# Conditioned attention on one core: the last three of 32 steps written out with four score banks, and the opening in another order

## The chip, the cores and the metric

The kernel runs on one core of one Trainium2 chip. The metric is the device time of one execution in microseconds (us), lower is better. The median of three runs before the change is 683.97 us (683.66 to 684.18).

## The reference

For each of 8 batch entries `x` is 512 tokens by 512 features, in 16 heads of 32. A condition vector is projected with the same weights and added to queries and keys (not to values). All in float32.

```python
Q = _split_heads(x @ Wq.T + bq)
K = _split_heads(x @ Wk.T + bk)
V = _split_heads(x @ Wv.T + bv)
cQ = Q + _split_heads(tokens @ Wq.T + bq)
cK = K + _split_heads(tokens @ Wk.T + bk)
scores = jnp.einsum('bhqd,bhkd->bhqk', cQ, cK) / jnp.sqrt(jnp.float32(HEAD_DIM))
attn = jax.nn.softmax(scores, axis=-1)
out = jnp.einsum('bhqk,bhkd->bhqd', attn, V)
x = x + out
```

## The kernel before, in words

**Tiling.** A group `g` is one batch entry and four heads, G = 32 groups. Everything is kept with features on the partitions. A projection is 12 products of 128x512: the float32 operand is split into a high part (rounded, `Wh`, `Xh`) and a low part (the rest, `Wl`, `Xl`), and high by high, low by high and high by low are added up over four chunks. The projected Q and K are split again into `hi` (`qk_hi`, ACT) and `lo` (`qk_lo`, DVE), and DMAs on SP's queue (`stack`) lay these out as rows of `Qs` and `Ks`, in three slots. A score tile then is one product over 96 rows.

**A group's work.** (1) `maxima`: 16 products of 128x512 in turn into two PSUM banks `MXB`, and on DVE one `row_maxima` each (L538), to find each query's maximum. POOL splits the maxima (`parts`), DVE turns them (`maxima_turned`), and four DMAs (`maxima_rows`, L757) put them under the queries as two more rows. (2) `scores`: 16 products over 98 rows (L291) in turn into two banks `STB`; ACT writes the exponentials to `Pt` (`exps`, L454), chunk by chunk of keys, four heads to a chunk. (3) `values`: per key chunk four products of V by `Pt` (L306), 16 in all and each recorded twice, into a bank of `OB`. (4) The sums: POOL adds the four chunks of `Pt` to `A` (`add`, L692, three additions of 128x2048), DVE `key_sums` reduces A (L551), PE `totals` (L314) finishes them. (5) DVE finishes: `sums_inverted`, `inverse_turned`, `normalised`, `added` (L559, L570, L580, L589), and SP stores.

**Order.** Every engine's order is written out by hand, and engines wait for each other on semaphores only. Step `t` of the loop interleaves on PE the 16 scores of group t with 16 maxima that are 9 tiles ahead of group t+1's beginning, with the 36 products of the three projections of group t+3, and, after score 1, with `totals(t-2)` and all of `values(t-1)`. From step 29 (G - 3) on there are no projections, and in steps 30 and 31 few or no maxima; the loop goes on as it is, with special code in step 31 (`last_adds`, `last_values`, `last_sums`), where the sums of the last group come from ones-products on PE. The projections' two banks `RB` are not used in these steps.

**Opening.** It projects q0, k0, q1, k1 one after the other, with the small `condition` and `condition_sum` products between, then interleaves 25 maxima tiles with v0, v1, v2, q2 and k2. The ACT order is L456 to L489, the DVE order L601 to L627. The weight chunks 2 and 3 of Wq and Wk are loaded on SP's queue (L788) and cast on ACT by `w_hi` (L406). `qk_hi(1, 1)` stands ahead of these casts (L477), and `qk_lo(1, 1)` behind the third row maximum (`K1_LO_AT`, L620).

## Time and profile before

| | |
|---|---|
| median of 3 runs | 683.97 us (683.66 to 684.18) |
| profiled execution | 683.72 us, its span 681.9 us |
| PE, DVE, POOL, ACT busy | 666.1, 542.1, 491.1, 376.0 us |
| mean granted clock of PE | 0.985 of full speed |
| chain that ended last | PE 92%, DMA 3%, DVE 2% |

PE is TensorE (PEld its weight loads), DVE VectorE, ACT ScalarE, POOL GpSimd, SP the engine whose queue issues the DMAs. A row of the timeline gives the start in the span, the duration, the engine, the line and operation, what is written from what, and in brackets how long the engine stood idle before and who released it. A row with xN merges N neighbours. The chain is followed back from the last instruction to what released it.

### The profile page before, as it was taken

The numbers are of one execution on the slowest core, as the hardware profiler recorded it, in microseconds if no ns is written. First come the engines' busy times: TensorE is split into PE (matmuls) and PEld (weight loads), VectorE is DVE, ScalarE is ACT, GpSimd is POOL, SyncE is SP. The second block draws the span as 40 slices with busy tenths as digits, with TensorE's granted clock in tenths as the row PEclk, the third lists the DMA queues.
The fourth block names the chain that finished last, engine by engine and source line by source line (L and its number), as shares of the span: only waits on it lengthen the run. The fifth ranks groups of instructions, "written<-read, shape, count | busy, mean of one in ns | idle before, by whom it ended". The sixth has DMA issues, their size and how long they took to land.

```text
span 681.9 us, 10057 instructions
## 1 busy us (share of the span) xinstructions
PE 666.1 (98%) x3534; PEld 451.0 (66%) x3534; DVE 542.1 (80%) x819; ACT 376.0 (55%) x659; POOL 491.1 (72%) x205
## 2 busy tenths in 40 slices
PE   8999999999999999999999999999999999999976
PEld 6776677666677666667766666776666677665521
DVE  4676888888888888888888888888888888888836
ACT  6335655555566555555655555565555555555552
POOL 6518777778877777887777798777779776667880
PEclk9999999999999999999999999999999999999878
DMA  7944334555343455533345553334554333444111
GB/s 242 237 109 99 89 105 100 139 140 141 99 116 98 109 139 140 134 101 112 100 116 141 139 129 99 112 96 127 140 140 121 82 97 91 123 125 125 33 48 46
DMA packets 48274, 79.85 MB, mean 117 GB/s; under 512 B 9824, under 2 KB 9824, under 8 KB 48224
## 3 DMA queue, kind: packets, MB, share of 16 engines
q1 hardware_dynamic: 47696, 79.19, 43.6%
q8 instruction: 28, 0.46, 0.3%
q14 instruction: 22, 0.18, 0.1%
q10 hardware_dynamic: 528, 0.02, 0.0%
HBM read 19.95 MB, written 8.39 MB: 42 GB/s over the span
## 4 chain that ended last, share of the span: by engine, by line
PE 92%; DMA 3%; DVE 2%; ACT 1%; SPq 1%; issue 1%; ACTq 0%; DVEq 0%
PE bank L198 25%; PE bank L291 18%; PE bank L276 17%; PE bank L306 16%; PE bank L254 13%; PE bank L314 1%; DVE mf L538 1%; ACT Pt L454 1%; DMA Ks<-lo 1%; DMA xr<-xT 1%; PE bank L323 1%; DMA cT<-condT 1%; DMA Qs<-mt 1%; SPq L757 0%; SPq L744 0%
## 5 line engine op out<-in xcount | busy, mean ns | idle before, releaser
L454 ACT ACTIVATE Pt<-bank 128x512 f32<-128x512 f32 x512 | 301.6, 599 | 238.2 <-PE bank L291 157.1
L538 DVE TENSOR_REDUCE mf<-bank 128x1 f32<-128x512 f32 x512 | 344.8, 686 | 106.6 <-PE bank L276 105.4
L692 POOL TENSOR_TENSOR A<-A,Pt 128x2048 f32<-128x2048 f32 x62 | 284.6, 4590 | 4.9
L291 PE MATMUL bank<-Qs,Ks 98*128 98x512 f32 x512 | 212.4, 417 | 4.6 <-ACT Pt L454 2.8
L276 PE MATMUL bank<-Ks,Qs 96*128 96x512 f32 x512 | 208.5, 407 | 1.8 <-DMA Ks<-lo 1.3
L692 POOL TENSOR_TENSOR A<-Pt 128x2048 f32<-128x2048 f32 x31 | 142.9, 4609 | 4.0 <-DVE part_sums L551 4.0
L291 PEld LDWEIGHTS bank<-Qs,Ks 98*128 98x128 f32 x512 | 97.6, 191 | 69.8 <-ACT Pt L454 46.4
L674 POOL TENSOR_TENSOR Xl<-xr,Xh 128x512 fp32r<-128x512 f32 x28 | 36.1, 1292 | 119.6 <-ACT Xh L422 119.6
L276 PEld LDWEIGHTS bank<-Ks,Qs 96*128 96x128 f32 x512 | 97.6, 191 | 28.4 <-DVE mf L538 5.2
L306 PE MATMUL bank<-Pt,V 128*32 128x512 f32 x992 | 114.2, 600 | 0.0
L198 PE MATMUL bank<-Xl,Wh 128*128 128x512 f32 x256 | 102.4, 400 | 0.0
L198 PE MATMUL bank<-Xh,Wl 128*128 128x512 f32 x256 | 102.1, 399 | 0.0
L198 PE MATMUL bank<-Xh,Wh 128*128 128x512 f32 x256 | 101.9, 398 | 0.0
L551 DVE TRANSPOSE_TENSOR_REDUCE part_sums<-A 128x32 f32<-128x1024 f32 x62 | 76.4, 1234 | 5.9 <-POOL A L692 5.9
L306 PEld LDWEIGHTS bank<-Pt,V 128*32 128x32 f32 x992 | 34.6, 110 | 52.7 <-issue 52.7
L198 PEld LDWEIGHTS bank<-Xh,Wh 128*128 128x128 f32 x256 | 48.9, 191 | 12.1 <-issue 0.8
L198 PEld LDWEIGHTS bank<-Xh,Wl 128*128 128x128 f32 x256 | 49.0, 192 | 11.2
L198 PEld LDWEIGHTS bank<-Xl,Wh 128*128 128x128 f32 x256 | 49.1, 192 | 10.8
L529 DVE SCALAR_TENSOR_TENSOR lo<-bank,tb,hi 128x512 fp32r<-128x512 f32 x64 | 47.6, 743 | 6.3 <-ACT hi L437 6.3
L254 PE MATMUL bank<-Wl,Xh 128*128 128x512 f32 x128 | 51.0, 399 | 0.0
L254 PE MATMUL bank<-Wh,Xl 128*128 128x512 f32 x128 | 51.0, 399 | 0.0
L254 PE MATMUL bank<-Wh,Xh 128*128 128x512 f32 x128 | 50.4, 394 | 0.0
(55 smaller groups left out, 328.5 us busy)
## 6 DMA issues: line engine op xcount, KB each, us to landing
Qs<-hi SPq DMA_DIRECT2D x64, 256.0 KB, 3.6
Ks<-hi SPq DMA_DIRECT2D x64, 256.0 KB, 3.6
Qs<-lo SPq DMA_DIRECT2D x32, 256.0 KB, 4.1
Ks<-lo SPq DMA_DIRECT2D x32, 256.0 KB, 4.0
res<-xT SPq DMA_DIRECT2D x32, 256.0 KB, 2.9
outT<-ot SPq DMA_DIRECT2D x32, 256.0 KB, 3.8
xr<-xT SPq DMA_DIRECT2D x28, 256.0 KB, 2.7
Qs<-mt SPq DMA_DIRECT2D x128, 4.0 KB
```

Source lines behind the costliest of these rows:

```text
L198: m = e.matmul(ring_bank(use)[:, :], w[:, qk, c, kc * P:(kc + 1) * P], x[:, b % 2, kc, :], start=(n == 0), stop=(n == 11))
L254: m = e.matmul(ring_bank(use)[:, :], x[:, b % 2, kc, c * P:(c + 1) * P], w[:, 2, kc, :], start=(n == 0), stop=(n == 11))
L276: e.matmul(MXB[u % 2][:, :], Qs[0:96, sl, j, qc * P:(qc + 1) * P], Ks[0:96, sl, j, :], start=True, stop=True).then_inc(t_mx, 1)
L291: e.matmul(STB[u % 2][:, :], Ks[0:98, sl, j, kc * P:(kc + 1) * P], Qs[0:98, sl, j, :], start=True, stop=True).then_inc(t_st, 1)
L306: m = e.matmul(OB[g % 2][32 * j:32 * j + 32, :], V[:, b % 2, kc, h * HD:(h + 1) * HD], Pt[:, kc, j, :], start=(kc == 0), stop=(kc == KC - 1))
L314: m = e.matmul(bk[32 * j:32 * j + 32, 0:16], sel[:, :], part_sums[:, j, :], start=True, stop=True)
L454: e.activation(Pt[:, kc, j, :], STB[u % 2][:, :], ACT.Exp, scale=SCALE).then_inc(a_e, 1)
L529: e.scalar_tensor_tensor(lo[:, qk, :], ring_bank(("qk"[qk], g))[:, :], tb[:, qk, c, b:b + 1], hi[:, qk, :].bitcast(F32), ALU.add, ALU.subt ...
L538: e.reduce_max(mf[:, g % 2, 4 * j + qc:4 * j + qc + 1], MXB[u % 2][:, :], AXX).then_inc(v_mx, 1)
L551: e.tensor_reduce(part_sums[:, 2 * i:2 * i + 2, :].rearrange("p j n -> p (j n)"), A[:, 2 * i:2 * i + 2, :].rearrange("p j (n i) -> p (j n) ...
L674: e.tensor_tensor(Xl[:, b % 2, kc, :], xr[:, n % 2, :], Xh[:, b % 2, kc, :].bitcast(F32), ALU.subtract).then_inc(p_x, 1)
L692: e.tensor_tensor(A[:, :, :], Pt[:, 0, :, :] if kc == 1 else A[:, :, :], Pt[:, kc, :, :], ALU.add).then_inc(p_a, 1)
```

## The change

The opening: on PE `condition_sum(1, 0)` comes after product 5 of k0's projection, not after 8. On ACT `qk_hi(1, 1)` comes after the four `w_hi` casts, on DVE `qk_lo(1, 1)` right after its bias and ahead of all row maxima.

The last three steps leave the loop and are written out. In step 29 all 23 maxima tiles that remain are done, two to a score. From group 30 on scores go to four banks (`STB` and `RB`). The value products of groups 29, 30 and 31 run in halves or smaller. The sums of groups 30 and 31 come from ones-products (`last_sums`): one addition on DVE (`add_first`) of chunks 0 and 1, and three ones-products per head. The sums of groups 29 and 31 are held in the part of `V` that is no longer needed; the residual rows of groups 30 and 31 are loaded early into `hi` and `xr`, and the last output has a buffer of its own. On DVE `key_sums` of group 28 comes after step 29's maxima.

```diff
@@ -20,7 +20,6 @@
 SCALE = float(HD) ** -0.5
 FIN = 4
 WARM = 3
-K1_LO_AT = 2
@@ -35,7 +34,11 @@
 Q_LO_AT, K_LO_AT = 11, 17
 FINISH_AT = (1, 1, 1, 1)
 SUMS_AT = (4, 6)
-LAST_AT = (9, 10, 11, 12)
+TAIL_MAXIMA = (1, 1, 2, 2, 2, 2, 2, 2, 2, 2, 2, 2, 1, 0, 0, 0)
+EARLY_AT, LATE_AT, LAST_SUMS_AT = 11, 3, 6
...
@@ -153,6 +156,24 @@
         def freed(use):
             kind, g = use
             return {"q": (v_lo, 2 * g + 1), "k": (v_lo, 2 * g + 2), "v": (a_v, g + 1)}[kind]
+        def st_bank(u):
+            return (STB + RB)[u % 4] if u >= SLOTS * (G - 2) else STB[u % 2]
+        def added_up(g):
+            return V[:, 0, :, :] if g in (G - 3, G - 1) else A
+        def res_rows(g):
+            if g < G - 2:
+                return res[:, :]
+            return hi[:, 0, :].bitcast(F32) if g == G - 2 else xr[:, 0, :]
+        def out_rows(g):
+            return ot[:, :] if g < G - 1 else xr[:, 1, :]
         def st_unit(g, kc, j):
...
@@ -284,20 +305,25 @@
                     if g < NSLOT:
                         e.wait_ge(p_ks, g + 1)
                 u = SLOTS * g + n
-                if u >= 2:
+                if u < 2:
+                    e.wait_ge(a_tc, 5 + u)
+                elif u < SLOTS * (G - 2) + 2:
                     e.wait_ge(a_e, u - 1)
+                elif u < SLOTS * (G - 2) + 4:
+                    e.wait_ge(v_lo, 2 * G)
+                    e.wait_ge(a_v, G)
                 else:
-                    e.wait_ge(a_tc, 5 + u)
-                e.matmul(STB[u % 2][:, :], Ks[0:98, sl, j, kc * P:(kc + 1) * P], Qs[0:98, sl, j, :],
+                    e.wait_ge(a_e, u - 3)
+                e.matmul(st_bank(u)[:, :], Ks[0:98, sl, j, kc * P:(kc + 1) * P], Qs[0:98, sl, j, :],
                          start=True, stop=True).then_inc(t_st, 1)
-            def values(g):
+            def values(g, chunks):
                 b, c = divmod(g, KC)
-                if g >= 2:
+                if g >= 2 and chunks[0] == 0:
                     e.wait_ge(v_f, finished(g - 2, FIN))
                 if g == 0:
                     e.wait_ge(v_tb, 6)
-                for kc in range(KC):
+                for kc in chunks:
                     if c == 0:
                         e.wait_ge(a_v, KC * b + kc + 1)
...
@@ -314,26 +340,18 @@
                     m = e.matmul(bk[32 * j:32 * j + 32, 0:16], sel[:, :], part_sums[:, j, :], start=True, stop=True)
                 m.then_inc(t_l, 1)
...
+                    m = e.matmul(bk[32 * j:32 * j + 32, :], ones[:, :],
+                                 added_up(g)[:, j, :] if kc is None else Pt[:, kc, j, :],
+                                 start=(kc is None), stop=(kc == KC - 1))
                 if kc == KC - 1:
-                    m.then_inc(t_last, 1)
-            def last_sums():
-                e.wait_ge(v_a, 2)
-                for j in range(4):
-                    e.matmul(MXB[1][32 * j:32 * j + 32, :], ones[:, :], A[:, j, :], start=True, stop=False)
-                e.wait_ge(a_e, st_unit(G - 1, KC - 1, 3))
-                for j in range(4):
-                    m = e.matmul(MXB[1][32 * j:32 * j + 32, :], ones[:, :], Pt[:, KC - 1, j, :],
-                                 start=False, stop=True)
-                m.then_inc(t_last, 1)
+                    m.then_inc(t_l, 1)
             warm_up()
@@ -345,7 +363,7 @@
             condition(1, 0)
             for n in range(12):
                 project_qk(1, 0, n)
-                if n == 8:
+                if n == 5:
                     condition_sum(1, 0)
             condition(0, 1)
             condition(1, 1)
@@ -372,32 +390,61 @@
             for k, g, n in first[done:]:
                 project(k, g, n)
...
-                    if u < SLOTS * G:
-                        maxima(u, t - 2 if n == VALUES_AT + 1 and t >= 2 else None)
+                    maxima(u, t - 2 if n == VALUES_AT + 1 and t >= 2 else None)
                     for k, g, i in work[done:done + PROJ[n]]:
                         project(k, g, i)
                     done += PROJ[n]
                     if n == VALUES_AT and t >= 1:
                         if t >= 2:
-                            e.wait_ge(v_mx, min(u, SLOTS * G))
+                            e.wait_ge(v_mx, u)
                             totals(t - 2, MXB[(u + 1) % 2])
-                        values(t - 1)
-                    if t == G - 1 and n == LAST_AT[0]:
-                        e.wait_ge(v_f, finished(G - 3, 1))
-                        totals(G - 2, MXB[0])
-                    if t == G - 1 and n == LAST_AT[3]:
-                        last_values(0)
-                        last_values(1)
-            last_values(2)
-            last_sums()
-            last_values(3)
+                        values(t - 1, range(KC))
+            u = SLOTS * (G - 2) + MAX_LEAD
+            for n in range(SLOTS):
+                scores(G - 3, n)
+                for i in range(TAIL_MAXIMA[n]):
+                    maxima(u, G - 5 if n == VALUES_AT + 1 and i == 0 else None)
+                    u += 1
+                if n == VALUES_AT:
+                    e.wait_ge(v_mx, u - 1)
+                    totals(G - 5, MXB[u % 2])
+                    values(G - 4, range(KC))
+                if n == EARLY_AT + 1:
+                    values(G - 3, (0, 1))
+            for n in range(SLOTS):
+                scores(G - 2, n)
+                if n == LATE_AT:
+                    values(G - 3, (2, 3))
+                    e.wait_ge(v_mx, SLOTS * G)
+                    totals(G - 4, MXB[0])
+                if n == EARLY_AT:
+                    values(G - 2, (0, 1))
+            for n in range(SLOTS):
+                scores(G - 1, n)
+                if n == LATE_AT:
+                    values(G - 2, (2, 3))
+                    e.wait_ge(v_f, finished(G - 4, 1))
+                    totals(G - 3, MXB[0])
+                if n == LAST_SUMS_AT:
+                    for kc in (None, 2, 3):
+                        last_sums(G - 2, MXB[1], kc)
+                if n == EARLY_AT:
+                    values(G - 1, (0, 1))
+            values(G - 1, (2,))
+            e.wait_ge(v_f, finished(G - 3, 1))
+            for kc in (None, 2, 3):
+                last_sums(G - 1, MXB[0], kc)
+            values(G - 1, (3,))
...
@@ -449,9 +496,14 @@
                 u = SLOTS * g + n
                 if j == 0 and g >= 1:
                     e.wait_ge(t_pv, KC * (g - 1) + kc + 1)
-                    e.wait_ge(p_a, 3 * (g - 1) + max(kc, 1))
+                    if g == G - 1 and kc < 2:
+                        e.wait_ge(v_a, 1)
+                    elif g == G - 1:
+                        e.wait_ge(t_l, G - 1)
+                    else:
+                        e.wait_ge(p_a, 3 * (g - 1) + max(kc, 1))
                 e.wait_ge(t_st, u + 1)
-                e.activation(Pt[:, kc, j, :], STB[u % 2][:, :], ACT.Exp, scale=SCALE).then_inc(a_e, 1)
+                e.activation(Pt[:, kc, j, :], st_bank(u)[:, :], ACT.Exp, scale=SCALE).then_inc(a_e, 1)
             e.wait_ge(v_c, 1)
             e.dma_start(cT[:, :, 0:B], condT).then_inc(d_c, 16)
@@ -474,10 +526,10 @@
             wv_hi(2)
             wv_hi(3)
             qk_hi(0, 1)
-            qk_hi(1, 1)
             for c in (2, 3):
                 w_hi(0, c)
                 w_hi(1, c)
+            qk_hi(1, 1)
             copy_part(0, 2)
             copy_part(1, 2)
...
@@ -558,11 +610,11 @@
                     e.wait_ge(v_f, finished(g - 1, FIN))
                 e.reciprocal(rc[:, :], bk[:, 0:16]).then_inc(v_f, 1)
-            def last_sums_inverted():
-                e.wait_ge(t_last, 1)
...
             def added(g):
                 O = OB[g % 2]
                 c = g % KC
                 e.wait_ge(v_f, finished(g, 3))
-                e.wait_ge(d_res, 16 * (g + 1))
-                if g >= 1:
+                if g < G - 2:
+                    e.wait_ge(d_res, 16 * (g + 1))
+                else:
+                    e.wait_ge(d_res_last, 32)
+                if 1 <= g < G - 1:
                     e.wait_ge(d_out, 16 * g)
-                e.scalar_tensor_tensor(ot[:, :], O[:, :], bqk[:, 2, c:c + 1], res[:, :],
+                e.scalar_tensor_tensor(out_rows(g), O[:, :], bqk[:, 2, c:c + 1], res_rows(g),
                                        ALU.add, ALU.add).then_inc(v_f, 1)
-            def last_adds(kc):
-                if kc == 1:
-                    e.wait_ge(v_s, 2 * (G - 1))
-                e.wait_ge(a_e, st_unit(G - 1, kc, 3))
-                if kc == 2:
-                    e.wait_ge(v_a, 1)
-                e.tensor_tensor(A[:, :, :], Pt[:, 0, :, :] if kc == 1 else A[:, :, :], Pt[:, kc, :, :],
-                                ALU.add).then_inc(v_a, 1)
+            def add_first(g):
+                e.wait_ge(v_s, 2 * (g - 1) if g == G - 1 else 2 * (G - 3))
+                e.wait_ge(a_e, st_unit(g, 1, 3))
+                e.tensor_tensor(added_up(g)[:, :, :], Pt[:, 0, :, :], Pt[:, 1, :, :], ALU.add).then_inc(v_a, 1)
             e.memset(cT[:, :, :], 0.0).then_inc(v_c, 1)
...
@@ -613,12 +661,9 @@
             for g in (0, 1):
                 for qk in (0, 1):
                     bias(qk, g)
-                    if (qk, g) != (1, 1):
-                        qk_lo(qk, g)
+                    qk_lo(qk, g)
             for u in range(SLOTS + MAX_LEAD):
                 row_maxima(u)
-                if u == K1_LO_AT:
-                    qk_lo(1, 1)
                 if u in (7, 8):
                     bias(u - 7, 2)
                 if u == SLOTS + 3:
@@ -626,11 +671,9 @@
             for qk in (0, 1):
                 qk_lo(qk, 2)
-            for t in range(G):
+            for t in range(G - 3):
                 for n in range(SLOTS):
-                    u = SLOTS * (t + 1) + n + MAX_LEAD
-                    if u < SLOTS * G:
-                        row_maxima(u)
+                    row_maxima(SLOTS * (t + 1) + n + MAX_LEAD)
                     if (g := due(t, n, TURN_AT, 1, 1)) is not None:
                         maxima_turned(g)
...
-                            normalised(G - 2)
-                        if n == LAST_AT[3]:
-                            added(G - 2)
-                        if n == 15:
-                            last_adds(2)
-            last_sums_inverted()
+            u = SLOTS * (G - 2) + MAX_LEAD
+            for n in range(SLOTS):
+                for i in range(TAIL_MAXIMA[n]):
+                    row_maxima(u)
+                    u += 1
+                if n == VALUES_AT:
+                    sums_inverted(G - 5, MXB[u % 2])
+                    inverse_turned(G - 5)
+                    normalised(G - 5)
+                    added(G - 5)
+                    qk_lo(1, G - 1)
+                if n == 6:
+                    maxima_turned(G - 2)
+            maxima_turned(G - 1)
+            key_sums(G - 4, 0)
+            key_sums(G - 4, 1)
+            sums_inverted(G - 4, MXB[0])
+            inverse_turned(G - 4)
+            normalised(G - 4)
+            added(G - 4)
+            add_first(G - 2)
+            key_sums(G - 3, 0)
+            key_sums(G - 3, 1)
+            sums_inverted(G - 3, MXB[0])
+            inverse_turned(G - 3)
+            normalised(G - 3)
+            added(G - 3)
+            last_sums_inverted(G - 2, MXB[1])
+            inverse_turned(G - 2)
+            add_first(G - 1)
+            normalised(G - 2)
+            added(G - 2)
+            last_sums_inverted(G - 1, MXB[0])
             inverse_turned(G - 1)
             normalised(G - 1)
...
@@ -684,12 +748,15 @@
                                 ALU.subtract).then_inc(p_ml, 1)
             def add(g, kc):
-                if kc == 1 and g >= 1:
+                if kc == 1 and g == G - 3:
+                    e.wait_ge(t_pv, KC * (G - KC))
+                elif kc == 1 and g >= 1:
                     e.wait_ge(v_s, 2 * g)
                 if kc > 1:
                     e.wait_ge(p_a, 3 * g + kc - 1)
                 e.wait_ge(a_e, st_unit(g, kc, 3))
-                e.tensor_tensor(A[:, :, :], Pt[:, 0, :, :] if kc == 1 else A[:, :, :], Pt[:, kc, :, :],
+                sums = added_up(g)
+                e.tensor_tensor(sums[:, :, :], Pt[:, 0, :, :] if kc == 1 else sums[:, :, :], Pt[:, kc, :, :],
                                 ALU.add).then_inc(p_a, 1)
             e.memset(sel[:, :], 0.0).then_inc(p_sel, 1)
@@ -715,16 +782,21 @@
             parts(0)
             x_lo(1, 2)
-            for t in range(G):
+            for t in range(G - 3):
                 if t >= 1:
                     add(t - 1, 3)
                 b, kc = divmod(t + 3, KC)
                 if b + 1 < B:
                     x_lo(b + 1, kc)
-                if t < G - 1:
-                    parts(t + 1)
-                    add(t, 1)
-                    add(t, 2)
+                parts(t + 1)
+                add(t, 1)
+                add(t, 2)
+            add(G - 4, 3)
+            parts(G - 2)
+            add(G - 3, 1)
+            parts(G - 1)
+            add(G - 3, 2)
+            add(G - 3, 3)
...
@@ -765,14 +837,17 @@
             def load_res(g):
                 b, c = divmod(g, KC)
-                if g >= 1:
+                if g >= G - 2:
+                    e.wait_ge(d_st[(G - 1) % NSLOT][0], 16 * 3 * ((G - 1) // NSLOT + 1))
+                    e.wait_ge(p_x, KC * (B - 1))
+                elif g >= 1:
                     e.wait_ge(v_f, finished(g - 1, FIN))
-                e.dma_start(res[:, :], xT[b, c * P:(c + 1) * P, :]).then_inc(d_res, 16)
+                e.dma_start(res_rows(g), xT[b, c * P:(c + 1) * P, :]).then_inc(d_res if g < G - 2 else d_res_last, 16)
...
                 if t >= 2:
                     store(t - 2)
-                if t + 1 < G:
-                    maxima_rows(t + 1)
-            for g in (G - 2, G - 1):
-                load_res(g)
+                maxima_rows(t + 1)
+            load_res(G - 4)
+            maxima_rows(G - 1)
+            load_res(G - 2)
+            load_res(G - 1)
+            store(G - 4)
+            load_res(G - 3)
+            for g in (G - 3, G - 2, G - 1):
                 store(g)
             e.wait_ge(d_out, 16 * G)
```

## Rows read from the trace of the kernel before

**Rows 1.** The page: the chain that ended last, and POOL's additions (section 5).
```profile
PE 92%; DMA 3%; DVE 2%; ACT 1%; SPq 1%; issue 1%; ACTq 0%; DVEq 0%
L692 POOL TENSOR_TENSOR A<-A,Pt 128x2048 f32<-128x2048 f32 x62 | 284.6, 4590 | 4.9
```
**Rows 2.** Timeline, the value products of four steps.
```profile
602.14 3.64 PE L306 MATMUL bank<-Pt,V 128*32 128x512 f32 x32
622.12 3.64 PE L306 MATMUL bank<-Pt,V 128*32 128x512 f32 x32
639.77 3.64 PE L306 MATMUL bank<-Pt,V 128*32 128x512 f32 x32
654.77 5.02 PE L306 MATMUL bank<-Pt,V 128*32 128x512 f32 x32
```
**Rows 3.** Timeline, waits in the last three steps.
```profile
626.47 1.97 DVE L538 TENSOR_REDUCE mf<-bank 128x1 f32<-128x512 f32 x3 [0.83 <-PE bank L276]
630.35 0.77 PE L276 MATMUL bank<-Ks,Qs 96*128 96x512 f32 x1 [1.11 <-DMA Ks<-lo]
632.54 0.79 PE L276 MATMUL bank<-Ks,Qs 96*128 96x512 f32 x1
653.49 1.22 PE L291 MATMUL bank<-Qs,Ks 98*128 98x512 f32 x2 [1.51 <-DMA Qs<-mt]
656.75 1.09 ACT L454 ACTIVATE Pt<-bank 128x512 f32<-128x512 f32 x2 [4.13 <-PE bank L306]
```
**Rows 4.** Stretches: us, then engines' busy time, PEclk (granted clock), DMA share, GB/s.
```profile
630.00:631.00 1.00, 0.65 (x2) 0.58 (x3) 1.00 (x3) 0.00 (x0) 0.17 (x1) 0.66 0.05 18
637.00:638.00 1.00, 1.00 (x4) 0.43 (x2) 0.98 (x2) 0.79 (x2) 1.00 (x1) 0.92 0.04 6
650.00:651.00 1.00, 0.73 (x2) 0.34 (x2) 0.00 (x0) 0.94 (x2) 1.00 (x1) 0.90 0.00 0
657.00:658.00 1.00, 1.00 (x12) 0.29 (x8) 0.55 (x1) 0.84 (x2) 1.00 (x1) 0.68 0.00 0
30.00:40.00 10.00, 10.00 (x44) 8.10 (x44) 8.60 (x14) 1.72 (x3) 1.71 (x3) 1.00 0.22 51
```
**Rows 5.** Timeline of the opening, ACT's `qk_hi(1, 0)`.
```profile
14.12 0.69 ACT L437 ACTIVATE hi<-bank,tb 128x512 fp32r<-128x512 f32 x1 [1.07 <-PE bank L198]
```
**Rows 6.** Timeline of the opening: weight loads, casts, `qk_hi(1, 1)`, maxima, `qk_lo(1, 1)`.
```profile
16.72 0.61 SPq L732 DMA_DIRECT2D Pt<-wqT  x1
18.34 0.44 SPq L732 DMA_DIRECT2D Pt<-wkT  x1
20.96 0.69 ACT L437 ACTIVATE hi<-bank,tb 128x512 fp32r<-128x512 f32 x1 [2.39 <-DMA Ks<-lo]
21.55 2.62 ACT L406 ACTIVATE Wh<-Pt 128x512 fp32r<-128x512 f32 x4
22.53 0.40 PE L276 MATMUL bank<-Ks,Qs 96*128 96x512 f32 x1
23.57 0.74 DVE L529 SCALAR_TENSOR_TENSOR lo<-bank,tb,hi 128x512 fp32r<-128x512 f32 x1
```
**Rows 7.** DMA issues of 16.6 to 18.6: KB each, median us to landing.
```profile
Pt<-wqT SPq DMA_DIRECT2D x2, 256.0 KB, 4.9
```
**Rows 8.** Timeline, pace of maxima and exps, the end of step 29, DVE's addition.
```profile
619.16 3.38 DVE L538 TENSOR_REDUCE mf<-bank 128x1 f32<-128x512 f32 x5 [0.16 <-PE bank L276]
637.21 1.12 ACT L454 ACTIVATE Pt<-bank 128x512 f32<-128x512 f32 x2 [0.26 <-PE bank L291]
645.14 4.74 ACT L454 ACTIVATE Pt<-bank 128x512 f32<-128x512 f32 x8 [0.18 <-PE bank L291]
665.86 2.29 DVE L598 TENSOR_TENSOR A<-Pt 128x2048 f32<-128x2048 f32 x1
```
**Rows 9.** The chain that ended last, near its end: start, us, what.
```profile
674.35 0.86 PE bank L331 x8
676.13 0.73 DVE rr L564
```

More of the change, by code:

```diff
@@ L95, in cond_attention @@
         d_res = sem("d_res")
+        d_res_last = sem("d_res_last")
         d_out = sem("d_out")
@@ L373, in tensor_program @@
                 project(k, g, n)
-            for t in range(G):
-                work = [(k, t + 3, n) for k in "vqk" if t + 3 < G for n in range(12)]
+            for t in range(G - 3):
+                work = [(k, t + 3, n) for k in "vqk" for n in range(12)]
                 done = 0
@@ L551, in key_sums @@
                 e.tensor_reduce(part_sums[:, 2 * i:2 * i + 2, :].rearrange("p j n -> p (j n)"),
-                                A[:, 2 * i:2 * i + 2, :].rearrange("p j (n i) -> p (j n) i", i=32), AXX, ALU.add,
+                                added_up(g)[:, 2 * i:2 * i + 2, :].rearrange("p j (n i) -> p (j n) i", i=32), AXX, ALU.add,
                                 apply_transpose=True).then_inc(v_s, 1)
@@ L716, in pool_program @@
             x_lo(1, 2)
-            for t in range(G):
+            for t in range(G - 3):
                 if t >= 1:
@@ L774, in store @@
                 e.wait_ge(v_f, finished(g, FIN))
[L775 removed]
+                e.dma_start(outT[b, c * P:(c + 1) * P, :], out_rows(g)).then_inc(d_out, 16)
             load_x0(0)
@@ L798, in sync_program @@
             stack(1, 2)
-            for t in range(G):
+            for t in range(G - 2):
                 b, kc = divmod(t + 3, KC)
@@ L805, in sync_program @@
                     load_res(t - 2)
-                if t >= 1 and t + 2 < G:
+                if t >= 1:
                     stack(0, t + 2)
```

34 lines of the change are left out of this document (11 added, 23 removed).

## The prediction, made before the changed kernel ran

> **What bounds the kernel now.** I read the page first. The matrix engine (PE) holds 92% of the chain that ended last [rows 1], so one step of the loop lasts as long as PE's own work. The timeline gives its length: the 32 records of the value products start at 602.14 and again at 622.12 [rows 2], a step of 19.98 us. In this regime no other engine's saving shows. That leaves the two ends, where PE is not the limit all the time. I read both as timelines and then as one-microsecond stretches for the granted clock.
>
> In the last three steps the projections are over. Value products start at 622.12, 639.77 and 654.77 [rows 2], so the steps are 17.7 and 15.0 us, and the rest from 654.77 to the span's end takes 27.1. Each time they run, ACT, which has two score banks only, runs dry: 4.13 us before 656.75 [rows 3]. PE also idled 1.11 us for the K rows of the last group before 630.35, and 1.51 for the maxima rows before 653.49 [rows 3]. And its clock fell three times to half (1.2 GHz): in the stretches that begin at 630 and 650, and it came back at 637 and 657 [rows 4]; a third fall, at 664 to 671, looks the same. Each lasted some 7 us.
>
> **The opening (three edits).** The moved `condition_sum(1, 0)` runs three matmuls earlier. Its consumer, `qk_hi(1, 0)` at 14.12, is released by the projection's end and not by the bias [rows 5]. I cost it at nothing; the cover is the projection itself. If the copy that it reads were late, PE would wait up to the 0.7 us of the three matmuls.
>
> `qk_hi(1, 1)` goes behind four casts of weight chunks on ACT. Now it runs at 20.96 and the casts take 2.62 us from 21.55 [rows 6]. Could the casts run in ACT's idle time before 20.96? No: their loads are issued from 16.72 to 18.34 [rows 6] and take 4.9 us to land [rows 7], which is 21.6 for the first and 23.2 for the last. So the casts stay where they are and end at 24.17, and `qk_hi(1, 1)`, 0.69 long, ends at 24.86 instead of 21.65.
>
> `qk_lo(1, 1)` on DVE goes from behind three row maxima to ahead of all of them. Queued behind its wait are all 25 row maxima of group 0 and the start of group 1, and PE waits for these: maxima tile 2 uses the bank of tile 0. On DVE the lower part takes 0.74 [rows 6], so it ends at about 25.65, the first maximum at 26.34, and PE's third maxima product goes from 22.53 [rows 6] to 26.4: **+3.9 us**. Nothing gives this back. From 30 to 40 PE is busy 10.00 of 10 us [rows 4], and the whole loop hangs on it by the step length above.
>
> The stall has a second price. PE would stand about 3.7 us. In the tail a stand of 1.11 us after sparse scores was enough for the clock to be at half when it went on [rows 3, 4]. PE then works at half rate where it is the bound. If the fall comes during the stall and ends near 33, 6.6 us run at half rate: **+3.3 us**. Bounds: the fall from 650 to 657 ended 3.0 us after PE's dense run of value products began at 654.77 [rows 3, 4], which would be +1.5 here; two falls in a row would be +6.6, and no fall would be 0. I take +3.3 because this stretch is not dense either: `condition` and `condition_sum`, small products that wait for copies, cut into it. Opening together: **+7.2 us** (3.9 to 10.5).
>
> The Trainium skill ("TensorE: Matmul & The Clock Gate", section "HAM oscillation — how this bites in real kernels") says that a wait between groups of matmuls can throttle the array, so that the next group starts cold. The trace agrees at 630 [rows 4]. By a reading that only the wait itself counts, the opening would cost 3.9; by the rule, the sum above.
>
> **The tail (one rewrite).** I walk it from 626.04, up to which nothing changes, in the old kernel's times. Step 29 now holds all 23 remaining maxima tiles instead of 16. From 626.47 [rows 3] on DVE has 21 to do; back to back one costs 0.68 (3.38 for five [rows 8]).
>
> - Five are done by 629.9. The next is the first of group 31 and waits for the same K rows as before: PE idles again till 630.35, and the clock falls again.
> - At half clock two banks give a reduction about every 0.78 us: the 0.79 of a product after a wait [rows 3], 0.69 for its reduction, 0.08 of hand-over, over two banks. Sixteen take from 631.2 to about 643.7 (643.0 at full clock).
> - The price: scores are interleaved one to two maxima. PE comes to the first half of `values(29)` at 642.8. At half clock a half takes 3.5 us (the full one 3.64 at full clock [rows 2]), so score 13 starts at 646.3 and the exps of step 29 end at 648.7. Before, they ended at 638.3 [rows 8]. The step is 10 us longer.
> - From there ACT can run nearly without a gap: eight exps take 4.74 us [rows 8], 9.5 for a step, against 15.0 now. Four banks cover 2.4 us of PE's absence and a half of the values is 1.8 at full clock. With `totals(28)` and the latency of the next score ACT idles 0.8 in step 30. It idles 0.4 behind the second half in step 31, and 1.5 at `last_sums(30)`: twelve ones-products, each group of four 0.86 [rows 9], stand between scores 6 and 7.
> - ACT's exps for step 30 then start at 648.7, and the last of step 31 ends at 671: 32 at 0.59, and 2.7 to 3.5 of such gaps.
> - The end: `last_sums` for chunk 3 comes 1.6 us behind the last exp, as PE still has the values of chunk 2 and two groups of sums to do. From the transposition to the end of the span it was 5.8 us (676.13 to 681.9 [rows 9]) and stays that. The span of the tail ends at 678.2: **-3.7 us**.
>
> Covers. POOL: `add(29, 2)` goes behind `parts(31)`, so it starts at 644 and the third addition ends at 653.3 (4.59 each [rows 1]); exp 12 of step 30 waits for it and comes at 655, cover 1.7. DVE: `add_first(30)`, 2.29 [rows 8], is needed by the first exp of step 31 (659) and ends at 657. The score rows for group 31 are there about 4 us behind the last reduction, at 648, seven before they are used. SP: `load_res(30)` and `load_res(31)` stand ahead of `store(28)` and `load_res(29)`, all waits behind them long over; buffers `hi` and `xr` are idle then, cost nothing. The other output rows cost nothing.
>
> Bounds of the tail: at full clock from 640 on, -5.4 (676.5). If the clock stays at half through the second half of `values(29)` too, the exps of step 29 end 0.5 later and ACT's gap behind that half is 3.2 instead of 0.8: 681.1, a gain of 0.8 only.
>
> The Trainium skill ("SBUF — State Buffer", "Who interferes with whom") says that a VectorE instruction with two SBUF inputs contends with a GpSimd instruction that reads SBUF. No row here shows the two at once: the two DVE additions of the tail (2.29 and 2.28) started after POOL's last one had ended. With it the sum would grow by what the third rival below gives.
>
> **The sum.** +7.2 - 3.7 = +3.5. The profiled execution took 683.72 (span 681.9, 1.8 around it), 0.25 below the median of 683.97. So 687.2 against its own time, 687.4 against the median.
>
> **Rivals.**
> - *The clock holds in the opening, and the tail runs at full clock* (the side of faster). Place: PE's stall at 22.7 to 26.4. Price 3.9 only; the tail's rewrite gives 5.4. That is -1.5: 682.4. Against it: all three sparse stretches of the tail lost the clock [rows 4]. It decides from the point where the opening costs less than the tail gives. Chance 0.13. With the tail at -3.7 it is +0.2, 684.2: no change, chance 0.12.
> - *Long half-clock spells, or late sums.* The opening costs 10.5, or the tail gives 0.8. Step 29 is then the bound that replaced PE: DVE's 21 reductions push everything behind them. +6.4 to +9.7: 690.4 to 693.7. For it: at half clock PE has more to do per exp and misses more of them, as at 650 to 657 [rows 4]; against it: the dense values end such a spell. Chance 0.2.
> - *DVE and POOL get in each other's way.* `add_first(30)` at 654 meets a late `add(29, 3)`: up to 2.3 more on DVE, of which the 2 us of cover take most; then the sums of group 29 come late at `totals(29)`: +1 to +2, 689. Chance 0.05, worked out from the DVE row of 2.29 and the POOL row of 4.59 [rows 1]. The rule of the Trainium skill quoted above is this one.
> - *The change does not do what it says*: ACT still runs dry at each block of values because bank four comes too late. Tail 0, total +7.2: 691.2, counted with the second rival.
>
> **How the numbers follow.** The forecast, 685.4 to 690.4 (the opening's low bound with the likeliest tail, up to one spell more), has 0.5 and is the likeliest. Faster by over 0.2% is below 682.6 and slower is above 685.3 (about what a measurement of this kernel can tell from no change). Faster 0.13, same 0.12, slower 0.75. The range leaves out the worst of the long spells and the best of the first rival: 682.5 to 692.0.
>
> **What would show it.** In the opening: the third maxima product at 26.4 instead of 22.5, `qk_hi(1, 1)` behind the casts at 24.2, matmuls at 0.63 instead of 0.40 till about 33, and the value products of every later step shifted by one constant. If they are shifted by less than 3, the DVE or landing term fails; if by 4, the clock term. In the tail: a last reduction near 643.5 plus the shift, steps 30 and 31 of about 11 us each, ACT almost gapless in them, and the distance from the value products of step 29 (622.12 now) to the end of the span 3.7 us shorter than 59.8. The forecast is wrong if the casts find their loads landed early, or if the tail, paced by DVE and not by PE, holds the clock.

## The result, and the profile after

The changed kernel takes 687.53 us (median of 5 runs, 686.1 to 688.28) against 684.18 for the old one: ratio 1.0045, 95% interval 1.0027 to 1.0062. It is slower, by 3.35 us; forecast were +3.5 and 687.4. Line numbers are those of each kernel: L297 is the maxima product (L276 before), L317 the score (L291), L332 the value product (L306), L506 the exp (L454).

The page of the changed kernel, span and chain:

```profile
span 686.5 us, 10100 instructions
PE 94%; DMA 2%; DVE 1%; ACT 1%; SPq 1%; issue 0%; ACTq 0%
```

The opening in its timeline (start, duration, engine, line, operation, idle time and releaser), to be laid beside [rows 6]:

```profile
21.84 0.40 PE L297 MATMUL bank<-Ks,Qs 96*128 96x512 f32 x1
25.19 0.63 ACT L453 ACTIVATE Wh<-Pt 128x512 fp32r<-128x512 f32 x1 [0.48 <-DMA Pt<-wkT]
25.73 0.67 ACT L484 ACTIVATE hi<-bank,tb 128x512 fp32r<-128x512 f32 x1
26.43 0.75 DVE L581 SCALAR_TENSOR_TENSOR lo<-bank,tb,hi 128x512 fp32r<-128x512 f32 x1 [6.82 <-ACT hi L484]
27.10 1.28 DVE L590 TENSOR_REDUCE mf<-bank 128x1 f32<-128x512 f32 x2
27.84 0.80 PE L297 MATMUL bank<-Ks,Qs 96*128 96x512 f32 x1 [5.13 <-DVE mf L590]
```

This is the chain of the forecast, read from top to bottom: the last cast waits for its load, the high part of k1 stands behind the cast, the low part waits 6.82 us on DVE, the row maxima stand behind it, and PE's third maxima product starts at 27.84 instead of 22.53 after standing 5.13 us. The loads were slower than before. The DMA view of the same stretch, KB each and median us to landing:

```profile
Pt<-wqT SPq DMA_DIRECT2D x2, 256.0 KB, 5.9
```

That is 1.0 more than [rows 7], and the stall is 1.4 longer than forecast (27.84 - 22.53 = 5.3 against 3.9). The clock, by stretches of one microsecond (PEclk is the third number from the end; compare [rows 4]):

```profile
25.00:26.00 1.00, 0.00 (x0) 0.00 (x0) 0.00 (x0) 0.81 (x2) 1.00 (x2) 0.95 1.08 227
32.00:33.00 1.00, 1.00 (x10) 0.20 (x8) 0.46 (x1) 0.00 (x0) 0.00 (x0) 0.63 0.06 25
636.00:637.00 1.00, 0.09 (x1) 0.00 (x0) 0.81 (x2) 0.36 (x1) 0.12 (x1) 0.94 0.77 256
653.00:654.00 1.00, 1.00 (x6) 0.50 (x2) 0.61 (x1) 0.00 (x0) 1.00 (x1) 0.52 0.03 4
```

It fell to half during the stall, at 25.9, and came back at 32.7. In the tail it fell at 636.9, and came back only at 654: one spell of 17 us in place of three of 7.

The tail in the timeline, beside [rows 2, 3, 8]:

```profile
629.22 3.64 PE L332 MATMUL bank<-Pt,V 128*32 128x512 f32 x32
637.07 0.77 PE L297 MATMUL bank<-Ks,Qs 96*128 96x512 f32 x1 [0.98 <-DMA Ks<-lo]
646.03 1.36 PE L297 MATMUL bank<-Ks,Qs 96*128 96x512 f32 x2
649.75 3.64 PE L332 MATMUL bank<-Pt,V 128*32 128x512 f32 x16
654.14 1.08 ACT L506 ACTIVATE Pt<-bank 128x512 f32<-128x512 f32 x2 [4.04 <-PE bank L317]
659.38 4.03 ACT L506 ACTIVATE Pt<-bank 128x512 f32<-128x512 f32 x8 [1.30 <-PE bank L317]
664.39 4.03 ACT L506 ACTIVATE Pt<-bank 128x512 f32<-128x512 f32 x8 [0.98 <-PE bank L317]
672.98 2.56 ACT L506 ACTIVATE Pt<-bank 128x512 f32<-128x512 f32 x5 [1.95 <-PE bank L317]
676.54 2.07 ACT L506 ACTIVATE Pt<-bank 128x512 f32<-128x512 f32 x4 [1.00 <-PE bank L317]
680.75 0.72 DVE L616 STREAM_TRANSPOSE rr<-bank 128x512 f32<-128x512 f32 x1 [2.84 <-PE bank L350]
```

The value products of step 29 start at 629.22, 7.10 later than in [rows 2]: that is all that the opening costs. The first product of q2's projection, near the end of the opening, was 7.56 late, so 0.46 came back in between:

```profile
43.69 0.40 PE L219 MATMUL bank<-Xh,Wh 128*128 128x512 f32 x1
```

against this line of the old kernel:

```profile
36.13 0.40 PE L198 MATMUL bank<-Xh,Wh 128*128 128x512 f32 x1
```

From the value products of step 29 to the end of the span it is 57.3 us against 59.8 before: the tail gives 2.5. So +7.1 - 2.5 = +4.6, and the spans differ by 4.6 (686.5 and 681.9). Half of the value products (x16) now takes 3.64 us at 649.75, as long as all 32 records took before: half clock. Behind it ACT runs groups of eight exps in 4.03 us.

Two lengths carry the rest of this document. The **shift** is the start of the value products of step 29 less 622.12. The **tail** is the time from there to the end of the span.

### The profile page after: what moved, and what is told of

Read it like the earlier page. It is cut to its first block, busy times and chain, and to the rows that moved or that the text cites. A ratio compares the mean times of both kernels' runs of the same rounds, so it can differ in the third digit from the quotient of the medians.

```text
span 686.5 us, 10100 instructions
## 1 busy us (share of the span) xinstructions
PE 670.6 (98%) x3558; PEld 451.9 (66%) x3558; DVE 541.4 (79%) x818; ACT 374.6 (55%) x659; POOL 477.6 (70%) x202
## 4 chain that ended last, share of the span: by engine, by line
PE 94%; DMA 2%; DVE 1%; ACT 1%; SPq 1%; issue 0%; ACTq 0%
PE bank L219 26%; PE bank L317 19%; PE bank L297 18%; PE bank L332 16%; PE bank L275 13%; DMA Pt<-wkT 1%; PE bank L340 1%; PE bank L350 1%; DMA cT<-condT 1%; DVE mf L590 1%; DMA Ks<-lo 0%; SPq L816 0%; ACT hi L484 0%; PE bank L248 0%; ACT Pt L506 0%
## 5 line engine op out<-in xcount | busy, mean ns | idle before, releaser
L506 ACT ACTIVATE Pt<-bank 128x512 f32<-128x512 f32 x512 | 300.4, 600 | 236.9 <-PE bank L317 162.8
L759 POOL TENSOR_TENSOR A<-A,Pt 128x2048 f32<-128x2048 f32 x58 | 266.5, 4595 | 4.5
L297 PE MATMUL bank<-Ks,Qs 96*128 96x512 f32 x512 | 211.4, 414 | 7.0 <-DVE mf L590 5.8
L317 PE MATMUL bank<-Qs,Ks 98*128 98x512 f32 x512 | 208.1, 412 | 1.0 <-ACT Pt L506 0.6
L317 PEld LDWEIGHTS bank<-Qs,Ks 98*128 98x128 f32 x512 | 97.1, 191 | 63.7 <-ACT Pt L506 42.5
L759 POOL TENSOR_TENSOR A<-Pt 128x2048 f32<-128x2048 f32 x29 | 133.8, 4613 | 2.7 <-DVE part_sums L603 2.7
L297 PEld LDWEIGHTS bank<-Ks,Qs 96*128 96x128 f32 x512 | 98.7, 193 | 37.6 <-DVE mf L590 14.9
L332 PE MATMUL bank<-Pt,V 128*32 128x512 f32 x1024 | 119.0, 602 | 0.0
L603 DVE TRANSPOSE_TENSOR_REDUCE part_sums<-A 128x32 f32<-128x1024 f32 x58 | 71.5, 1234 | 0.0
L332 PEld LDWEIGHTS bank<-Pt,V 128*32 128x32 f32 x1024 | 35.0, 110 | 54.3 <-issue 52.7
```

What stands on the lines that cost most here:

```text
L297: e.matmul(MXB[u % 2][:, :], Qs[0:96, sl, j, qc * P:(qc + 1) * P], Ks[0:96, sl, j, :], start=True, stop=True).then_inc(t_mx, 1)
L317: e.matmul(st_bank(u)[:, :], Ks[0:98, sl, j, kc * P:(kc + 1) * P], Qs[0:98, sl, j, :], start=True, stop=True).then_inc(t_st, 1)
L332: m = e.matmul(OB[g % 2][32 * j:32 * j + 32, :], V[:, b % 2, kc, h * HD:(h + 1) * HD], Pt[:, kc, j, :], start=(kc == 0), stop=(kc == KC - 1))
L506: e.activation(Pt[:, kc, j, :], st_bank(u)[:, :], ACT.Exp, scale=SCALE).then_inc(a_e, 1)
L603: e.tensor_reduce(part_sums[:, 2 * i:2 * i + 2, :].rearrange("p j n -> p (j n)"), added_up(g)[:, 2 * i:2 * i + 2, :].rearrange("p j (n i) ...
L759: e.tensor_tensor(sums[:, :, :], Pt[:, 0, :, :] if kc == 1 else sums[:, :, :], Pt[:, kc, :, :], ALU.add).then_inc(p_a, 1)
```

## The experiments

`K1_LO_AT`, `TAIL_MAXIMA` and the other names are those of the diff above. Ratios are against the old kernel.

**1. The two parts alone.** One kernel is the old one with the three opening edits, the other the new one with them undone:

```diff
             qk_hi(0, 1)
-            qk_hi(1, 1)
             for c in (2, 3):
                 w_hi(0, c)
                 w_hi(1, c)
+            qk_hi(1, 1)
```

(and `qk_lo(1, 1)` ahead of the row maxima, `condition_sum(1, 0)` after product 5.)

> The old kernel with the three opening edits alone. My theory (the stall of the matrix engine at its third maxima product, and the half-clock spell behind it, shift everything): value products of every step about 7.0 us later than in the old kernel, 691.0 us in all. Rival (the opening costs only the wait, about 4, and the tail's rewrite loses the rest): 688. Second rival (the opening costs nothing, the loss is all in the tail): 684.

Measured: 690.54, ratio 1.009 (1.0065 to 1.0115). Shift 6.46, tail 59.5. The third maxima product starts at 26.25, 3.72 late.

> The new kernel with the old opening: only the last three steps are rewritten. My theory: the tail gives 2.5 us as in the changed kernel's profile (value products of step 29 to the end of the span: 57.3 against 59.8), so 681.5. Rival (the tail gives nothing or loses, the opening is cheap): 684 or more. If the two parts add up, this ratio and that of the opening alone sum to the change's.

Measured: 681.30, ratio 0.995 (0.993 to 0.9971). Shift 0.1, tail 57.3, as in the changed kernel. The two parts add up: +0.9% and -0.5% give the change's +0.45%. The rivals in which the opening is cheap or the tail gives nothing have fallen.

**2. Which of the opening's edits?** Old kernel with only the ACT order of the diff above:

> The old kernel with only the cast order on ScalarE changed: the high part of k1 behind the four weight casts; the low part stays behind the third row maximum. My theory: VectorE waits for the high part after three maxima instead of none, so the matrix engine stands at its sixth maxima product, not at the third, and gets three tiles and six value projections done first: +1.5 to +3, 685.5 to 687. Rival (the cost is the late landing of the high and low rows of K, not VectorE's order): +7, 691.

Measured: 684.59, ratio 1.0002 (0.9987 to 1.0017). Less than the 685.5 to 687 that I expected. The profile has the mechanism: the sixth maxima product waits for DVE, not the third.

```profile
26.46 0.75 DVE L529 SCALAR_TENSOR_TENSOR lo<-bank,tb,hi 128x512 fp32r<-128x512 f32 x1 [2.78 <-ACT hi L437]
27.86 0.50 PE L276 MATMUL bank<-Ks,Qs 96*128 96x512 f32 x1 [0.89 <-DVE mf L538]
```

In this timeline PE stands 0.89 us, its clock stays at 1.00, and the low part is just as late as in the changed kernel (26.46 and 26.43). This profiled execution's weight loads took 7.1 us to land, among the longest of all, and its shift of 1.6 is more than the medians show. Now only DVE's order:

```diff
                     bias(qk, g)
-                    if (qk, g) != (1, 1):
-                        qk_lo(qk, g)
+                    qk_lo(qk, g)
...
                 row_maxima(u)
-                if u == K1_LO_AT:
-                    qk_lo(1, 1)
```

> The old kernel with only VectorE's order changed: the low part of k1 ahead of all row maxima, its high part early as before. My theory: the high part ends at 21.7, so the first row maximum is 0.9 late and the third maxima product 0.6 late: 0 to +0.6, within 0.2% of the old kernel, 684.0 to 684.6. Rival (the low part's place alone makes the stall): +4 or more.

Measured: 685.61, ratio 1.002 (1.0005 to 1.0035), a little over what I expected. The third maxima product starts at 22.99, 0.46 late, and the shift is 0.58; its tail was 61.4 in this profile, with the same code as before. So the edits alone measured +0.02% and +0.2% (at most 0.35% by the interval), and all three together 0.9%. The late high part costs nothing that the medians show as long as three row maxima stand ahead of the low part; the early low part costs about half a microsecond by the shift as long as the high part is early. The loss is the pair. The third edit, `condition_sum`, is in the kernel with 0.9% as well and was not tried alone. The traces leave it little: the second maxima product, which comes after it, starts at 21.84 with it and at 21.81 without.

**3. The wait or the clock?** The opening edits with 20 products that nobody reads (`FILL` is 20) in PE's standing time:

```diff
             for u in range(SLOTS + MAX_LEAD):
+                if u == 2:
+                    for _ in range(FILL):
+                        e.matmul(OB[1][:, :], Wh[:, 0, 0, 0:P], Xh[:, 0, 0, :], start=True, stop=True)
                 maxima(u)
```

> The opening edits alone, with 20 products that nobody reads (into a free bank) before the third maxima product, 4.3 us of work in the time in which the matrix engine stands. My theory: the stall stays as long as it was (the third maxima product still waits for VectorE), but the clock stays at 2.4 GHz, which takes 2 to 3 us from the loss: 688.0 against 690.5 for the opening without them. Rival (the half-clock spell costs nothing, the whole loss is the wait): 690.5.

Measured: 687.88, ratio 1.0056 (1.0034 to 1.0077): 2.7 us below the opening without them by the medians, 2.3 by the ratios, 2.4 by the shift (4.10 against 6.46). The granted clock stayed at 1.00 from 20 to 38. From the third maxima product to the first product of q2's projection it was 13.6 us, exactly as in the old kernel, and 16.4 in the opening without fillers. The half-clock spell costs 2.8 us there and 2.3 in the changed kernel (15.85, from 27.84 to 43.69). In the opening without fillers that leaves the wait: 3.7 + 2.8 is its shift of 6.46. With the fillers the comparison of shifts understates the clock a little, since they ran longer than DVE kept PE waiting:

```profile
22.49 4.70 PE L366 MATMUL bank<-Xh,Wh 128*128 128x512 f32 x20
25.48 1.28 DVE L542 TENSOR_REDUCE mf<-bank 128x1 f32<-128x512 f32 x2
```

The first row maximum was done at 26.2, and the third maxima product started at 27.03, behind the last filler: about 0.8 us are the fillers' own.

**4. What are four banks worth?** The new tail with `st_bank` returning `STB[u % 2]` throughout:

```diff
-            return (STB + RB)[u % 4] if u >= SLOTS * (G - 2) else STB[u % 2]
+            return STB[u % 2]
```

(and the wait in `scores` back to `a_e >= u - 1`.)

> The new tail on the old opening, with two score banks for the last two groups instead of four. My theory: four banks cover 2.4 us of the matrix engine's absence at each block of values and let the exps run at 0.50 each, as the changed kernel's profile has it, not at 0.59: without them the last two steps grow by 1 to 2 us each, 684 to 685, and ScalarE's idle time before the first exp behind a block is over 2 us. Rival (the matrix engine is the bound there and the banks are idle luxury): 681.3, as with four.

Measured: 690.3, ratio 1.0075 (1.0051 to 1.0099), tail 66.7. Nine us more than with four banks (9.4 by the tail); I had expected three to four. Its profile says where. ACT in its timeline:

```profile
645.87 2.97 ACT L502 ACTIVATE Pt<-bank 128x512 f32<-128x512 f32 x5 [3.42 <-PE bank L313]
653.18 2.27 ACT L502 ACTIVATE Pt<-bank 128x512 f32<-128x512 f32 x4 [2.85 <-PE bank L313]
668.75 1.78 ACT L502 ACTIVATE Pt<-bank 128x512 f32<-128x512 f32 x3 [3.86 <-PE bank L313]
```

and the granted clock (third number from the end) in steps 30 and 31:

```profile
648.00:649.00 1.00, 0.87 (x3) 0.40 (x2) 0.00 (x0) 0.84 (x2) 0.97 (x1) 0.67 1.01 373
662.00:663.00 1.00, 0.96 (x3) 0.45 (x2) 0.00 (x0) 0.79 (x2) 0.00 (x0) 0.50 0.06 16
668.00:669.00 1.00, 1.00 (x2) 0.34 (x2) 0.95 (x2) 0.25 (x1) 0.00 (x0) 0.58 0.00 0
```

ACT stands 2.85 to 3.86 us behind the blocks, an exp takes 0.59 (2.97 for five) and not 0.50, and PE, held back by ACT, lost its clock twice more. I had priced the waits and not the clock. Without the banks the rewritten tail is slower than the old one.

**5. Step 29 at full clock.** The new tail with 22 products that nobody reads (not 23, as the expectation has it): 17 between score and maxima (`TAIL_FILL`: one in slots 2 to 4, two in 5 to 11) and five (`K_FILL`) before the first maxima product of group 31:

```diff
                 scores(G - 3, n)
+                if n == 2:
+                    e.wait_ge(v_lo, 2 * G)
+                    e.wait_ge(a_v, G)
+                for _ in range(TAIL_FILL[n]):
+                    e.matmul(RB[0][:, :], Wh[:, 0, 0, 0:P], Xh[:, 1, 0, :], start=True, stop=True)
                 for i in range(TAIL_MAXIMA[n]):
+                    if u == SLOTS * (G - 1):
+                        for _ in range(K_FILL):
+                            e.matmul(RB[0][:, :], Wh[:, 0, 0, 0:P], Xh[:, 1, 0, :], start=True, stop=True)
                     maxima(u, G - 5 if n == VALUES_AT + 1 and i == 0 else None)
```

> The new tail on the old opening, with 23 extra products in step 29 that nobody reads (into a free projection bank), so that the matrix engine works through the wait for the last K rows and between the maxima. My theory: the clock stays at 2.4 GHz, a pair of maxima takes 1.4 us instead of 1.6, the first half of the values of group 29 takes 1.8 instead of 3.6: 3 to 3.6 us less, 678. Rival (the clock is no cost in a step that VectorE paces): 681.3 or more, as the extra products delay the maxima.

Measured: 677.43, ratio 0.9896 (0.9881 to 0.9911), 3.9 below the tail without them; measured a second time 677.58, ratio 0.9896 (0.9876 to 0.9916). Its tail is 53.9. The granted clock (third number from the end) in a stretch of step 29, and in the timeline the first half of the values of group 29:

```profile
628.00:640.00 12.00, 11.90 (x46) 7.61 (x44) 10.42 (x18) 4.78 (x8) 5.00 (x3) 1.00 0.22 56
```

```profile
640.84 1.92 PE L335 MATMUL bank<-Pt,V 128*32 128x512 f32 x16
```

The half takes 1.92 in place of 3.64, half of the 3.4 us that the tail got shorter. Nearly all of the rest lies ahead of it, in the faster pace of the maxima and of the products around them: from the value products of step 29 to this half it is 19.14 us, and 20.70 without the fillers.

**6. The K rows of the last group earlier.** `qk_hi(1, 31)` before the first exp of step 29, `qk_lo(1, 31)` before the finishing of group 27:

```diff
+                    if t == G - 3 and n == 0:
+                        qk_hi(1, G - 1)
                     exps(t, n)
...
                 if n == VALUES_AT:
+                    qk_lo(1, G - 1)
                     sums_inverted(G - 5, MXB[u % 2])
```

> The new tail on the old opening, with the high and low part of the last group's K made before the first exp of step 29 and before the finishing of group 27. My theory: its rows land 2.3 us earlier, so the 1.0 us wait for them is gone and VectorE's chain of maxima starts again 1 us earlier: -1.0 to -1.5, 680. If the wait alone made the clock fall, it holds and -3 more comes. Rival (the finishing, 0.7 later, holds something up): 681.3 or more.

Measured: 678.86, ratio 0.9915 (0.9898 to 0.9931): 2.4 below the tail without it, more than the 1.0 to 1.5 that I expected. In the profiled execution, the slowest of the four, the tail is 56.3, only 1.0 less; where the other 1.4 us come from is open. From its timeline:

```profile
629.60 0.47 PE L298 MATMUL bank<-Ks,Qs 96*128 96x512 f32 x1 [0.70 <-DMA Ks<-lo]
641.68 3.64 PE L333 MATMUL bank<-Pt,V 128*32 128x512 f32 x16
```

PE still waits 0.70 us for the rows. Their last DMA is issued at 623.44, and they are there at 629.5 only, 6 us; in the changed kernel it was 3.4 (the chain has it from 633.53 on):

```profile
623.44 6.02 DMA Ks<-lo
```

The clock fell all the same, at 632, 2.3 us after that wait had ended, in a stretch in which PE follows VectorE's pace with waits of 0.2 to 0.4 us between its products. So making the wait shorter did not save the clock. That the pace alone, without any wait for the rows, would lose it is likely but not shown: no kernel without fillers got rid of the wait.

> The new tail on the old opening with both edits: the last group's K made early and products that nobody reads in step 29. My theory: the two overlap in part. Filling took 3.6 us by keeping the clock, the early K about 2; with the clock kept, the early K still takes away most of VectorE's 0.76 us of waiting for the K rows: 676.6, 0.5 to 1 below the filled tail. Rival (both removed the same spell of half clock): 677.4, as filled alone.

Measured: 677.76, ratio 0.9899 (0.9878 to 0.9919), tail 53.9. As filled alone (53.9): the rival was right. It agrees with both edits having removed parts of the same spell, which lasted 17.1 us in the new tail and 13.6 with the early rows.

**7. Who is the bound in the last two steps?** First the gap of 1.95 us in ACT is broken up by spreading the ones-products, in the kernel with both edits of 6:

```diff
-                if n == LAST_SUMS_AT:
-                    for kc in (None, 2, 3):
-                        last_sums(G - 2, MXB[1], kc)
+                if n in (4, 5, 6):
+                    last_sums(G - 2, MXB[1], (None, 2, 3)[n - 4])
```

> The kernel with both edits, and the three groups of ones-products for the sums of group 30 behind scores 4, 5 and 6 instead of all behind score 6. My theory: in steps 30 and 31 the matrix engine itself is the bound (the chain there is nearly all its own work), so closing ScalarE's gap of 2.0 us behind these products gives nothing: within 0.5 us of the kernel with both edits. Rival (ScalarE's exps are the bound there, as my forecast had it): 1.5 us less.

Measured: 678.39, ratio 0.9912 (0.9895 to 0.9929), tail 54.6 against 53.9: no gain. ACT's timeline behind the ones-products:

```profile
661.25 0.60 ACT L516 ACTIVATE Pt<-bank 128x512 f32<-128x512 f32 x1 [0.74 <-PE bank L320]
662.67 0.60 ACT L516 ACTIVATE Pt<-bank 128x512 f32<-128x512 f32 x1 [0.82 <-PE bank L320]
664.09 2.56 ACT L516 ACTIVATE Pt<-bank 128x512 f32<-128x512 f32 x5 [0.83 <-PE bank L320]
```

The one gap has become three, each ended by a score of PE, and they are no shorter together. Then the same kernel as in 5 with less for PE to do; it leaves out the ones-products of chunk 2, so the sums of groups 30 and 31 lack a chunk:

```diff
-            for kc in (None, 2, 3):
+            for kc in (None, 3):
                 last_sums(G - 1, MXB[0], kc)
```

(and so for group G - 2.)

> The filled tail on the old opening, with the ones-products of chunk 2 left out for groups 30 and 31 (their sums lack a chunk): 8 products less on the matrix engine, 1.7 us by the groups of 0.86. My theory (the matrix engine is the bound from the values of group 29 to the last transposition): the whole 1.7 us goes, 1.5 to 1.8 less than the filled tail in the same call. Rival (ScalarE's exps are the bound in these steps, as in my forecast): only the part behind the last exp goes, 0.9 or less.

Measured: 675.95, ratio 0.9872 (0.9851 to 0.9893); its tail is 52.2, 1.7 below the 53.9 of the filled one, which was measured with it:

> The filled tail once more, for the comparison with the one with fewer ones-products on the same chip: 677.4, 1.0% under the old kernel.

Measured: 677.58, the second time of experiment 5.

Two groups of 0.86 taken away are 1.72, and 1.7 is gone. This alone does not decide between the two: the first group stood in a gap of ACT that PE made (it went from 1.95 to 1.09), and the second stands behind the last exp, so a chain that runs through ACT would have lost both as well. What decides is the spread sums, and the busy time of the engines in the changed kernel from 656 to 681 (PE first, ACT fourth):

```profile
656.00:681.00 25.00, 24.77 (x175) 9.37 (x175) 14.88 (x18) 16.32 (x32) 4.58 (x1) 1.00 0.16 56
```

PE is busy 24.77 of 25 us and ACT 16.32. PE, not ACT, is the bound there.

## Why the prediction was right

**The opening's stall: right, a size off.** Place, queue and order were as written. The wait was sized at 3.9 and came to 5.3 in the changed kernel, 3.7 in the opening alone. It goes with the load time of the weight chunks, 5.9 and 5.0 us by the median. I had taken 4.9 from one execution as if it were fixed; over the fourteen profiles of this stretch the medians of these loads lay between 4.3 and 7.4.

**The clock in the opening: right, a size off.** +3.3 was forecast, 2.25 and 2.8 measured (experiment 3), by a fall at 25.9 that ended at 32.7, where I had it end near 33. A third term was missing: I had written that nothing gives the stall back, and of 7.56 us at q2's projection 0.46 were given back by step 29. The three together, 5.3 + 2.25 - 0.46, make 7.1 against 7.2: the errors cancelled.

**`condition_sum`**: forecast at nothing. Shift and stall leave no remainder for it, and the second maxima product is 0.03 late, but it was not tried alone.

**Step 29: right.** In old times the first half of the values was to start at 642.8 and started at 649.75 - 7.10 = 642.65; the exps of the step were to end at 648.7 and ended at 655.93 - 7.10 = 648.83 (the end of an exp in the chain). A pair of maxima takes 1.58 us, forecast 1.56.

**The last two steps: the mechanism was wrong, the size nearly right.** I wrote that ACT can run nearly without a gap, at 0.59 each, with 2.7 to 3.5 us of gaps. The exps ran at 0.50, and the five gaps were 1.30, 0.98, 1.04, 1.95 and 1.00, 6.3 in all. The 0.59 of [rows 8] was not ACT's own pace but the round trip through two banks; experiment 4 has it again with two banks in the new tail. With four banks ACT is faster than PE can feed it, and PE's own work (scores, values and six groups of ones-products) fills the time. From the last exp of step 29 to the last of step 31 it was 22.7 us, 16.4 of exps and 6.3 of gaps; forecast were 18.9 + 3.1. That the sum is only 0.7 off is luck: each part missed by 2.5 or more, in opposite directions. From the last exp to the transposition it was 2.1 us, forecast 1.6. With the 0.1 of step 29 this is 1.2 to 1.3 us late: the tail gave 2.5 instead of 3.7.

**The rivals.** *The clock holds in the opening, and the tail runs at full clock*: did not happen by itself, but both halves are real. With fillers, experiment 3 has the first, and experiment 5 the second, at 53.9 or 5.9 less than before, where the bound said 5.4. *Long half-clock spells*: in the tail the spell lasted 17 us, but it ended before the second half of the values. *DVE and POOL*: not in the changed kernel, where POOL's last addition ended at 660.64 and DVE's began at 661.55. In the filled tail they met for 0.7 us, from 650.65 to 651.39. Its timeline has them:

```profile
650.65 2.89 DVE L658 TENSOR_TENSOR A<-Pt 128x2048 f32<-128x2048 f32 x1
642.16 9.23 POOL L773 TENSOR_TENSOR V<-V,Pt 128x2048 f32<-128x2048 f32 x2
```

The addition on DVE took 2.89 against 2.29 in [rows 8]. The Trainium skill says in "SBUF — State Buffer", "Who interferes with whom", that a VectorE instruction with two inputs in SBUF contends with a GpSimd instruction that reads SBUF; this row agrees, and so do the other four filled profiles (2.88 to 2.91). The cover took it whole: the addition ended at 653.5, and ACT's eight exps from 653.51 on, the fifth of which waits for it, have no gap. *The change does not do what it says*: fell with experiment 4: without the four banks the tail loses 6.9 us instead of giving 2.5.

**The median.** The profile's difference is 4.6 us, the medians' 3.35. Profiles of the old tail's code gave 59.5, 59.8, 59.9, 61.4 and 62.1. In the two long ones the value products of step 30 ran into a half-clock spell (4.66 and 5.31 us instead of 3.64), so a single profile is good to about 2 us here. The forecast's 687.4 against 687.53 is closer than its terms deserve: the opening's errors cancelled, the tail was 1.2 us off, and the distance between profile and median covered that. So the closeness of the total is luck; the direction and the opening's mechanism are not.

**What beats both.** The new tail on the old opening takes 681.3, and with fillers in step 29 677.4 to 677.6, 1.0% below the old kernel.

## What to carry to other kernels

An instruction moved behind a load on one engine, and its consumer moved to the head of another engine's queue, may each be nearly free and together cost a stall: price the pair, and add the clock to the wait. A busy time per instruction that was read from a loop through two banks is the loop's round trip; before four banks are priced with it, ask which engine is the bound once the round trip is gone. Where the matrix engine has to follow a slower engine for a whole step, as in step 29 here, work that nobody reads can be worth more than the wait that one tries to remove (3.9 us against 2.4).

## What the runs showed of the hardware

- Exps of 128x512 with the next tile already in PSUM follow each other every 0.50 us (eight in 4.03), though each is listed with 0.60.
- The clock fell without a long wait: in experiment 6 the longest was 0.70 us, in a stretch in which PE did a score and two maxima products each 1.4 us. At half clock the same pattern ran from 636.9 to 654 without the clock coming back, 17 us, until value products had run through.
- A load of 256 KB in the crowded opening (DMA share about 1.05) lands after 4.3 to 7.4 us, by the medians of fourteen profiles of kernels that issue the same loads in the same order.
- A VectorE addition of 128x2048 from two SBUF inputs that overlapped a GpSimd addition for 0.7 us took 2.9 us instead of 2.29, in all five filled profiles; the GpSimd additions kept their pace (two in 9.23, as in the old kernel's 9.24).
